# A second, transposed score pass in two attention stages of a gated cross-attention block

## The reference, cut to what matters

```python
x = x + tanh(g_xattn[0]) * L0_xattn(layernorm(x), ctx, ctx, ...)   # 64 heads of 16, all 128 keys, softmax
x = x + tanh(g_ffn[0])   * L0_ffn(layernorm(x), ...)               # dense plus low rank
x = x + tanh(g_xattn[1]) * L1_xattn(layernorm(x), ctx, ...)        # 8 heads of 16, a window of 16 keys out of 1024 positions
x = x + tanh(g_ffn[1])   * L1_ffn(layernorm(x), ...)               # dense, masked by clusters
```

## Time and profile before

| what | value |
|---|---|
| time, median of 3 runs | 2407.38 us (2406.6 to 2408.14) |
| the profiled execution's own time | 2407.05 us |
| its span | 2405.4 us |
| busy: PE, PE weight loads | 2182.1 us (91%), 1766.2 us (73%) |
| busy: DVE, ACT, POOL | 1394.1 us (58%), 975.4 us (41%), 174.0 us (7%) |
| DMA | 426.59 MB, mean 177 GB/s |

### The profile page before, as it was taken

One profiled execution on the slowest core, in us unless ns is written; L12 is line 12 of the kernel. 1 busy time (PEld: TensorE's weight loads), 2 busy tenths in 40 slices (PEclk: granted clock), 3 DMA queues, 4 the chain that ended last, 5 costly groups with the idle time before them and its releaser, 6 DMA issues. The chain is left out here.

```text
span 2405.4 us, 49290 instructions
## 1 busy us (share of the span) xinstructions
PE 2182.1 (91%) x17638; PEld 1766.2 (73%) x17638; DVE 1394.1 (58%) x2604; ACT 975.4 (41%) x2850; POOL 174.0 (7%) x225
## 2 busy tenths in 40 slices
PE   5999699999979999979978999959999996775998
PEld 4999689989957777758854777737777774564887
DVE  4443322112159999923325777649999995784664
ACT  2222221111059999900002111129999995440000
POOL 0000000000021212100000000010000000330000
PEclk9999899999989999989988999979999998886999
DMA  3223533332356777533323878775655653751221
GB/s 126 106 105 123 172 135 132 140 148 113 131 229 260 273 276 267 197 140 131 131 96 128 304 291 314 277 303 183 241 195 195 238 186 96 247 175 58 87 86 58
DMA packets 163583, 426.59 MB, mean 177 GB/s; under 512 B 14192, under 2 KB 90736, under 8 KB 151216
## 3 DMA queue, kind: packets, MB, share of 16 engines
q1 hardware_dynamic: 161200, 417.16, 47.2%
q0 software_dynamic: 2304, 8.39, 1.1%
HBM read 257.73 MB, written 167.77 MB: 177 GB/s over the span
## 5 line engine op out<-in xcount | busy, mean ns | idle before, releaser
L953 ACT ACTIVATE a_probs<-a_s_bank,a_nmax 128x128 f32<-128x128 f32 (+3 forms) x2176 | 598.8, 422 | 36.0 <-DVE a_nmax L893 36.0
L893 DVE TENSOR_REDUCE a_nmax<-a_s_bank 128x8 f32<-128x1024 f32 (+1 forms) x240 | 293.5, 1223 | 47.5 <-PE a_s_bank L999 23.8
L1009 PE MATMUL a_t_bank<-ident_sb,a_probs 128*128 128x128 f32 (+3 forms) x2176 | 286.2, 275 | 1.1 <-ACT a_pt L961 0.8
L1009 PEld LDWEIGHTS a_t_bank<-ident_sb,a_probs 128*128 128x128 f32 (+3 forms) x2176 | 225.0, 142 | 21.0 <-ACT a_probs L953 1.1
L907 DVE COPY a_pt<-a_t_bank 128x512 f32<-128x512 f32 (+3 forms) x272 | 177.1, 651 | 4.3 <-PE a_t_bank L1009 4.3
L961 ACT ACTIVATE a_pt<-a_t_bank 128x512 f32<-128x512 f32 (+3 forms) x272 | 165.0, 606 | 29.0 <-PE a_t_bank L1009 27.4
L1024 PE MATMUL a_o_bank<-a_pt,a_vpad 128*32 128x128 f32 (+3 forms) x4352 | 168.8, 273 | 0.5 <-DVE a_osb L914 0.5
L373 PE MATMUL q_qb<-q_xt_hi,wq_hi 128*128 128x256 f32 x512 | 145.5, 284 | 3.0 <-DVE wq_lo L248 3.0
L373 PE MATMUL kv_kb<-kv_ct_hi,wk_hi 128*128 128x256 f32 x512 | 145.0, 283 | 3.0 <-DVE wv_lo L248 3.0
L373 PE MATMUL kv_kb<-kv_ct_lo,wk_hi 128*128 128x256 f32 x512 | 144.9, 283 | 0.0
L373 PE MATMUL kv_kb<-kv_ct_hi,wk_lo 128*128 128x256 f32 x512 | 144.9, 283 | 0.0
(11 more groups left out here) (200 smaller groups left out, 4563.6 us busy)
## 6 DMA issues: line engine op xcount, KB each, us to landing
a_qs<-q SPq DMA_DIRECT2D x32, 1024.0 KB, 6.1
a_ks<-k SPq DMA_DIRECT2D x32, 1024.0 KB, 8.1
k<-f_shared SPq DMA_DIRECT2D x64, 512.0 KB, 4.2
a_qs<-q SPq DMA_DIRECT2D x16, 2048.0 KB, 7.8
a_ks<-k SPq DMA_DIRECT2D x16, 2048.0 KB, 11.9
k<-kv_raw SPq DMA_DIRECT2D x32, 512.0 KB, 4.8
k<-kv_k_lo SPq DMA_DIRECT2D x32, 512.0 KB, 4.8
a_vraw<-v SPq DMA_DIRECT2D x32, 512.0 KB, 10.4
```

What stands on the lines that cost most here:

```text
L893: dve.tensor_reduce(nmax[0:m, k, :], scores(s)[0:m], X, ALU.max, negate=True).then_inc(maxed, 1)
L953: a = act.activation(probs[0:m, k, h, :], scores(s)[0:m, h, :], ACT.Exp, bias=nmax[0:m, k, h:h + 1])
L1009: a = pe.transpose(t_bank[:, h // 4, h % 4 * P:h % 4 * P + m], probs[0:m, k, h, :], e.ident[0:m, 0:m])
```

## The change

Both attention stages compute the scores twice. The first pass (queries as rows, `score`) only serves the maxima. These are collected for a group of units (4 in layer 0, 3 in layer 1), transposed in one go (`turn_max`), copied by ACT and written by a DMA from ACT's queue into partitions 0 and 64 of qs (`shift`); the matching rows of k hold ones, written once in `setup`. The second pass (`score_t`) makes keys the rows, with the negated maximum already subtracted by that contraction row. One activation per unit then gives the transposed probabilities directly, so the transposes of the probabilities and their copies go. `value` multiplies them with the values and, in a second set of products, with a tile of ones, so that each output channel has its denominator beside it; `divide` takes the reciprocal of the whole 128-column tile and multiplies. Outputs are channel-major, and the transposes in the wo `gemm` and in `select` go. s_bank and o_bank have one buffer each (4 banks and 1 bank before: now 2 banks and 1), st_bank has two buffers of 2 banks. Tiles of layer 1 step by 112 positions instead of 113. The loads of q and k have four slots instead of two in layer 0 and layer 1. The constant START, the offset of all counters, goes from 16 to 32.

```diff
-TSTEP = P - WIN + 1
+TSTEP = P - WIN
...
+K_ROWS = ((0, slice(1, 16)), (0, slice(17, 32)), (1, slice(0, 32)), (2, slice(0, 32)), (3, slice(0, 32)))
+Q_ROWS = ((0, slice(0, 32)), (1, slice(0, 32)))
...
+            sp.wait_ge(unit_set, 1)
+            for k in (e.k0, e.k1):
+                sp.dma_start(k[:, 0:32:16, 0, :], unit[:]).then_inc(unit_out, 16)
+            sp.wait_ge(unit_out, 32)
...
+            pool.memset(unit[:], 1.0).then_inc(unit_set, 1)
...
-                    for j in range(4):
-                        sp.dma_start(e.k0[2 * g + b][:, j, :],
-                                     (k_hi, k_lo)[j % 2][:, b].rearrange("p o t -> p (o t)").bitcast(F32)
-                                     ).then_inc(k_out, 16)
+                    for j, r in K_ROWS:
+                        src = (k_lo, k_hi)[j % 2][4 * r.start:4 * r.stop, b].rearrange("p o t -> p (o t)")
+                        sp.dma_start(e.k0[2 * g + b][r, j, :], src.bitcast(F32)).then_inc(k_out, 16)
...
+        s_bank = ps(n + "s_bank", [P, 2, 512]); st_bank = ps(n + "st_bank", [P, 4, 512])
+        n_bank = ps(n + "n_bank", [P, 1, 512]); o_bank = ps(n + "o_bank", [P, 1, 512])
...
+            def divide(u, s, i):
+                m, k = un.rows(s), s % 2
                 dve.wait_ge(valued, done(u))
+                dve.reciprocal(rinv[:, k, 0:m], o_bank[:, 0, P:P + m]).then_inc(inv, 1)
+                dve.wait_ge(inv, u + 1)
...
+                dve.tensor_tensor(att[:, slot, to], o_bank[:, 0, 0:m], rinv[:, k, 0:m],
                                   ALU.mult).then_inc(normed, 1)
 
-            staggered(dve, B * upb, un.per_loop, [(4, maximum), (2, turn_out), (1, value_out), (0, divide)])
+            staggered(dve, B * upb, un.per_loop, [(0, divide), (L - 1, pads), (L + 1, maximum)])
...
+                act.wait_ge(st_done, done(u))
                 act.wait_ge(valued, free(u))
+                act.activation(pt[:, k, :, 0:m], by_head(st_bank[:, 2 * k:2 * k + 2, :])[:, :, 0:m],
+                               ACT.Exp).then_inc(expd, 1)
+
+            def shift(u, s, i):
+                if not un.group_last(s):
+                    return
+                g, k, mg = un.nth_group(s, i), s // G % 2, un.group_rows(s)
+                nth = un.groups // 2 * i + s // G // 2
+                act.wait_ge(turned, g + 1)
+                act.wait_ge(shift_in[k], 16 * shifts * nth)
+                act.activation(nrow[:, k, 0:mg], n_bank[0:R, 0, 0:mg], ACT.Copy).then_inc(rowed, 1)
+                act.wait_ge(rowed, g + 1)
+                if layer == 0:
+                    act.dma_start(qs[0:65:64, s // 4, :, :].bitcast(F32), nrow[:, k, :].bitcast(F32)).then_inc(shift_in[k], 16)
+                    return
+                for tile in range(G):
+                    slot, js, q, _ = place(s - s % G + tile)
+                    act.dma_start(qs[0:65:64, slot, :, q].bitcast(F32),
+                                  nrow[tile:R:G, k, 0:q.stop - q.start].bitcast(F32)).then_inc(shift_in[k], 16)
...
+            staggered(act, B * upb, un.per_loop, [(2, exponential), (L - 2, pads), (L, shift)])
...
+                pe.wait_ge(maxed, free(u, 1))
...
+            def turn_max(u, s, i):
+                if not un.group_last(s):
+                    return
+                g, mg = un.nth_group(s, i), un.group_rows(s)
+                pe.wait_ge(maxed, done(u))
+                pe.wait_ge(rowed, g)
+                pe.transpose(n_bank[0:R, 0, 0:mg], nmax[0:mg, s // G % 2, :], e.ident[0:mg, 0:mg]).then_inc(turned, 1)
+
+            def score_t(u, s, i):
+                slot, js, q, k = place(s)
+                m, st = un.rows(s), 2 * (s % 2)
+                if un.group_first(s):
+                    nth = un.groups // 2 * i + s // G // 2
+                    pe.wait_ge(shift_in[s // G % 2], 16 * shifts * (nth + 1))
                 pe.wait_ge(expd, free(u))
                 if layer == 1:
                     kind = {None: 1, 0: 0, 1: 2}[un.edge(s)]
                     for bank in range(2):
+                        pe.matmul(st_bank[:, st + bank, :].rearrange("p (h t) -> p h t", h=4)[:, :, 0:m], identb[:],
+                                  band[:, 1, kind, :, 0:m], start=True, stop=False, skip_group_check=True)
                 for j in range(4):
                     for half in range(2):
                         at = slice(64 * half, 64 * half + 64)
+                        a = pe.matmul(st_bank[:, st + half, j * P:j * P + m], ks[at, slot, js.start + j, k],
+                                      qs[at, slot, js.start + j, q], start=layer == 0, stop=True,
+                                      skip_group_check=True)
+                a.then_inc(st_done, 1)
...
+                pe.wait_ge(expd, done(u))
+                pe.wait_ge(normed, free(u, 1))
...
+                for half in range(2):
+                    at = slice(HD * half, HD * half + 2 * HD)
                     for j in range(4):
+                        pe.matmul(o_bank[32 * j:32 * j + 32, 0, 0:m], vz[:, slot, 4 * (s % upb) + j, at],
+                                  pt[:, k, 4 * half + j, 0:m], start=half == 0, stop=half == 1, skip_group_check=True)
+                for half in range(2):
+                    at = slice(HD * half, HD * half + 2 * HD)
+                    for j in range(4):
+                        a = pe.matmul(o_bank[32 * j:32 * j + 32, 0, P:P + m], ones[:, at],
+                                      pt[:, k, 4 * half + j, 0:m], start=half == 0, stop=half == 1 and ed is None,
+                                      skip_group_check=True)
+                if ed is not None:
+                    for j in range(4):
+                        a = pe.matmul(o_bank[32 * j:32 * j + 32, 0, P:P + m], pad_sel[:, j, :],
+                                      pad_exp[:, ed, 0:m], start=False, stop=True, skip_group_check=True)
                 a.then_inc(valued, 1)
...
-            staggered(pe, B * upb, un.per_loop, [(4, score), (2, turn), (1, value), (0, turn_back)])
+            staggered(pe, B * upb, un.per_loop, [(L + 1, score), (2, score_t), (1, value), (L, turn_max)])
...
-            staggered(pe, B, 4, [(0, first_half), (1, turn), (0, second_half)])
+            if ln_on:
+                staggered(pe, B, 4, [(0, first_half), (1, turn), (0, second_half)])
+            else:
+                staggered(pe, B, 4, [(0, first_half), (0, second_half)])
...
-            batches(act, [(3, projected), (4, attention_out), (2, rows_out), (1, exponential)])
+            batches(act, [(3, projected), (2, rows_out), (1, exponential)])
...
-            batches(pe, [(3, project), (4, turn_attention), (2, turn_rows), (1, logits)])
+            batches(pe, [(3, project), (2, turn_rows), (1, logits)])
```

435 lines of the change are left out of this document (203 added, 232 removed).

## The result

The changed kernel takes 2580.8 us (median of 4 runs, 2551.7 to 2613.1) against 2407.0 us. The sign was as predicted, the size was not: the median is 147 us above the forecast and 101 us above the range, and even the fastest run is 72 us above it. The profiled execution took 2594.45 us.

The account below looks back on a forecast made before the run. The o_bank loop was taken to bound the first attention, PE the second: 2407 - 15 (first attention) + 63 (second) - 15 (wo) - 4 (select) - 2 (stores) = 2434 us, range 2392 to 2480.

Parts of the forecast that it names:

- The sign: Whole kernel: the change makes it slower, 2434 us against 2407; chance of slower 0.7.
- nine filling steps: Start of the first attention: only scores and maxima run, at low clock, 2.4 us each, 22 us.
- o_bank loop: First attention: one buffer makes values and divide wait for each other, setting the step at 2.38 us.
- Rival 1: First attention: reciprocal takes 1.23 us instead of 0.87, loop 2.74, 43 us more, kernel 2477 us; chance 0.15.
- ones: Second attention, PE: four more value sets, multiplying by ones, add 0.40 us a step.
- band: Second attention, PE: a second band pass over 448 of 512 columns adds 0.48 us a step.
- pad products: Second attention, PE: four more products on two of nine units add 0.04 us a step.
- upper bound of 3.35: Second attention: most PE needs per step, with weight waits, small transpose and extra products; 3.2 us was taken.
- rival 4: First attention: the shift's DMA lands late, 5.9 us; 32 groups wait 1.4 us each, 45 us, kernel 2479; chance 0.08.
- Rivals 2 and 3: Both: PE switches cheaply, second attention's step 3.04 us; kernel 2386 us (chance 0.18) or, reciprocal as forecast, 2412 (chance 0.12).
- rival 2: Both attentions: PE alone sets the steps, 2.2 and 3.04 us, reciprocal cheap as a product; kernel 2386 us, chance 0.18.
- wo, ffn0 and the rest: Outside the attentions: wo gains 15 us without its transposes, select 4 us, the final stores 2 us.

Follow-up runs that it names:

- e5: Changed kernel plus two unused 128-row by 384-column products in every unit of the first attention: median 2528.1 us.
- e7: Changed kernel plus eight unused 128x128 transposes in every unit of the first attention: median 2652.7 us.
- e11: Changed kernel with the second attention and select of the kernel before, plus one unused 512-column product per unit of the first attention: 2420.1 us, ratio 1.006 against before.
- e6: Changed kernel plus three more pairs of score products (64 rows by 128 columns) in every unit of the first attention: median 2708.1 us.
- e9: Kernel before, with the first attention's transposes, except its first two units', replaced by 32-column products: runs of 2512, 2515, 2521, 2859 and 2872 us.
- e2: Changed kernel with a copy of the denominators in place of their reciprocal: 2581.3 us.
- e4: Kernel before, with only the second attention's loop written out over 36 units instead of 18: 2425.4 us against 2406.1, ratio 1.008.
- e18: e11 with ACT copying o_bank, POOL multiplying, second scores one unit further ahead, the unused product in st_bank, DVE's maximum before its reciprocal: 2450.2 us, ratio 1.015 against before.
- e13: e11 with ACT copying o_bank, DVE taking only the reciprocal, POOL the product, and the second score pass one unit further ahead: 2432.8 us, ratio 1.011 against before.
- e1: Changed kernel plus five unused 384-column products behind each of the nine score passes that fill the first attention's pipeline: median 2581.1 us.

## Why the prediction was wrong

**The step that failed: the clock.** The prediction said of the first attention that in the nine filling steps "the clock is low", and from there on counted 119 steps at full clock. The clock was low for 304 us instead, until 983.6 us: after the fill about 71 steps at 3.84 us on average instead of 2.57, 90 us. The prediction had taken's mean of 0.97 as a given of the stage. It hung on work that the change removes, the 8 transposes of 1.02 us together. e5, e7 and e11 (dense work back, clock up), e6 (more of the thin work, clock down) and e9 (the transposes of the old kernel made thin, clock down in two of five runs) show it from both sides. Open are two things: what it is about the transposes that holds the clock, since the pieces that the change adds stream their 128 columns in the same time at the low clock, and why a given run of a thin step settles high or low. No rival of the prediction had a low clock beyond the fill, so the time that came about had no chance of its own. But the sign did not hang on the clock: at 2.57 us throughout, the first attention would have taken about 442 - 90 = 352 us, against 340 before, where a gain of 14.5 was forecast.

**Mis-sized: the o_bank loop.** The mechanism was right (the waits between 1061 and 1064 us, and e2), though DVE by itself would have been only 0.15 us shorter. It measured 2.57 us and not 2.38: 0.99 from the reciprocal's start to the product's where I had 0.90, then 0.44 to PE's values (1062.00 to 1062.44) where I had 0.35, and 1.14 back to the reciprocal where I had 1.13. 0.19 x 127 steps = 24 us. With the clock's 90 that is 114 of the 116 us of the stage. Rival 1's 1.23 for the reciprocal was too much. The reciprocals by size:

```profile
L955 DVE RECIPROCAL a_rinv<-a_o_bank 128x128 f32<-128x128 f32 x128 | 122.6, 957 | 118.3 <-PE a_o_bank L1078 118.3
...
L955 DVE RECIPROCAL a_rinv<-a_o_bank 128x112 f32<-128x112 f32 x112 | 96.1, 858 | 88.7 <-PE a_o_bank L1078 88.7
```

6.2 ns for each further element, near the 5.6 of the earlier trace rows by which I had put 0.87 us for 128. The Trainium skill ("VectorE: DVE Perf Modes", walkthrough of the 8-slice pipeline) gives a repeat count of 8, by which I had estimated 1.07 us and more; the trace lies between it and the short rows, and decides.

**Missed: the loop body.** "The pipeline is nine steps deep" was read, `per_loop = 36` was not priced. By e4 it costs 19 us. In the changed kernel two stalls of 5.5 and 2.2 to 2.4 us each and the low clock behind them cost 25 us (the reciprocals there are 13.7 and 13.6 us apart, and the next ones up to 5.6, instead of 3.1). The start is most of the rest of the second attention's 32 us: the clock was low until 1734.5 us, 37 us after the first product, and the filling steps, counted at 27 us, were a few us longer.

**Right:** PE sets the second attention at 3.1 to 3.2 us a step, with 3.11 measured and 3.20 in the mean of nine units. Two of its terms were somewhat high (ones 0.34 for 0.40, band 0.37 for 0.48); the pad products were low (0.4 us in two of nine units, 0.09 a unit, for 0.04). The terms given for its upper bound of 3.35 add up to 3.40; nothing hung on it. ACT falls far below the others. The shift's DMA held up only a weight load at each stage's start, by 0.8 us or less, so rival 4 fell. Rivals 2 and 3 wanted PE's least sum, 3.04 us, in the second attention, and it took 3.20; rival 2 also wanted a reciprocal of 0.29, and it took 0.96. wo, ffn0 and the rest gained 10.4 us where 21 were forecast: wo's first product still comes 17.4 us after the last of the attention, 16.3 before, since the loads and the split stand there and not the transposes; select's and the stores' gains were 0.8 together.

The Trainium skill ("TensorE: Matmul & The Clock Gate", Part 1) says that the throttled state is the default and that activity releases it; the same page says of transposes (Part 4) that they don't count as busy in the same way. The first agrees with e5 and e11, where added work brought the clock up; but by itself it would not have given this result, since PE was noted as busy from 800 to 980 us in the changed kernel and the clock stayed low. The second, by which the old kernel's clock should have been the worse one, does not agree with e7: eight transposes a unit brought the clock to 1.00 and kept it there.

## What to carry to other kernels

Before you take work off TensorE, ask what holds its clock: a row that shows PE busy says nothing of it, the clock column of each stretch does. An engine can be occupied and slow at once, and then one long unused product may be worth its time, if it stands where the engine waits anyway (e11); where it does not, it costs its full time (e18). Price the length of a loop's body as you price its instructions, and look for idle time with no releaser at each jump back.

## What the runs showed of the hardware

PE at 100% busy and 1.2 GHz for 180 us (changed kernel) and for 760 us (e9). Two outcomes of one program: 2512 to 2521 and 2859 to 2872 us (e9). Eight transposes and eight pairs of score products take the same 1.90 us at 1.2 GHz, and the clock came up with the first (e7) and not with the second (e6). A product of 512 columns that stands alone between other groups took 0.43 us at 2.4 GHz (e18), a reciprocal of 128 elements a partition 0.96. Stalls at the jump back of a loop: none for a body of 16 units of the changed kernel, with one long product more (e11) or 18 of the old second attention; 4.2 us at two jumps of e13; 6.3 to 7.8 us with two long products or eight transposes more a unit, 5.3 us for 36 units of the old second attention and 5.5 and 2.2 to 2.4 for 36 of the new one. In e1 3.7 to 4.6 us appeared at the jumps of a body that had not been edited, with only the code ahead of it longer; that was not followed up.
